# Six block slots in the last pass of a graph network, and two split-precision layers for its first five chunks

## The reference

```python
x = layernorm(x + relu((adj @ x) @ L0_kernel + L0_bias))
u = x
for _ in range(3):
    v = mlp(adj @ u, uv weights)     # three layers, leaky ReLU (0.01) after each
    u = mlp(adj @ v, vu weights)
return layernorm(x + v)
```

## Time and profile before

| | us |
|---|---|
| time, median of 3 runs | 1171.17 |
| span of the profiled execution, first to last instruction | 1169.0 |
| outside of the span (1171.17 - 1169.0) | 2.2 |
| PE busy | 1154.0 (99%) |
| DVE busy | 738.2 (63%) |
| ACT busy | 660.8 (57%) |
| last pass (tick 1392 on), start in the trace | about 1037.9 |

### The profile page before, as it was taken

How to read it: one execution, slowest core, us unless ns; L and a number is a source line. 1 busy time by engine, 2 the same in 40 slices (tenths; PEclk the granted TensorE clock), 3 DMA queues, 4 the chain that set the end, 5 groups by cost and what they waited for, 6 DMA issues and landing times.

```text
span 1169.0 us, 13697 instructions
## 1 busy us (share of the span) xinstructions
PE 1154.0 (99%) x5236; PEld 953.1 (82%) x5236; DVE 738.2 (63%) x890; ACT 660.8 (57%) x809; POOL 0.2 (0%) x4
## 2 busy tenths in 40 slices
PE   7999999999999999999999999999999999999997
PEld 6888888888888888888888888888888888887776
DVE  7997676458564555555545756554566555658886
ACT  7765554346554555555444754554566454557885
POOL 0000000000000000000000000000000000000000
PEclk9999999999999999999999999999999999999999
DMA  9988775568466646555656736655665566569891
GB/s 383 405 299 327 244 270 192 206 215 288 124 207 209 215 161 214 198 185 180 216 180 216 250 118 216 214 173 181 210 222 188 190 205 209 193 217 362 296 323 50
DMA packets 72210, 261.60 MB, mean 224 GB/s; under 512 B 8017, under 2 KB 8657, under 8 KB 71121
## 3 DMA queue, kind: packets, MB, share of 16 engines
q1 hardware_dynamic: 72000, 260.61, 64.2%
q10 hardware_dynamic: 144, 0.13, 0.0%
HBM read 258.61 MB, written 2.10 MB: 223 GB/s over the span
## 4 chain that ended last, share of the span: by engine, by line
PE 92%; DMA 3%; DVE 2%; ACT 2%; issue 1%; SPq 0%; DVEq 0%; ACTq 0%
PE agg_ps L872 28%; PE agg_ps L865 28%; PE agg_ps L858 28%; PE pre_ps L769 4%; DMA adj_raw<-in_adj 3%; PE hid_ps L730 1%; PE hid_ps L732 1%; PE hid_ps L731 1%; DVE adj_lo L722 1%; ACT adj_hi L593 1%; PE hid_ps L791 1%; PE hid_ps L805 0%; DVE stats L606 0%; ACT hid L487 0%; ACT resid L508 0%
## 5 line engine op out<-in xcount | busy, mean ns | idle before, releaser
L722 DVE TENSOR_TENSOR adj_lo<-adj_raw,adj_hi 128x1024 fp32r<-128x1024 f32 x488 | 576.7, 1220 | 230.2 <-ACT adj_hi L593 224.0
L858 PE MATMUL agg_ps<-adj_hi,feat_hi 128*128 128x512 f32 x1532 | 607.7, 397 | 7.4 <-ACT adj_hi L593 7.4
L865 PE MATMUL agg_ps<-adj_hi,feat_lo 128*128 128x512 f32 x1532 | 598.0, 390 | 0.0
L593 ACT ACTIVATE adj_hi<-adj_raw 128x1024 fp32r<-128x1024 f32 x488 | 492.8, 1052 | 94.8 <-PE agg_ps L872 80.3
L872 PE MATMUL agg_ps<-adj_lo,feat_hi 128*128 128x512 f32 x1532 | 473.8, 390 | 0.2 <-DVE adj_lo L722 0.2
L858 PEld LDWEIGHTS agg_ps<-adj_hi,feat_hi 128*128 128x128 f32 x1532 | 288.5, 188 | 68.8 <-issue 10.2
L865 PEld LDWEIGHTS agg_ps<-adj_hi,feat_lo 128*128 128x128 f32 x1532 | 288.5, 188 | 62.2 <-issue 3.4
L872 PEld LDWEIGHTS agg_ps<-adj_lo,feat_hi 128*128 128x128 f32 x1532 | 287.8, 188 | 61.9 <-DVE adj_lo L722 1.5
L487 ACT ACTIVATE hid<-hid_ps,params 128x512 f32<-128x512 f32 (+1 forms) x80 | 54.5, 681 | 59.1 <-PE hid_ps L732 50.6
L558 ACT ACTIVATE in_hi<-part 128x512 fp32r<-128x512 f32 x24 | 15.2, 634 | 110.3 <-DVE part L711 110.3
L487 ACT ACTIVATE post<-pre 128x512 f32<-128x512 f32 x39 | 24.6, 630 | 79.8 <-DVE pre L689 79.8
(11 more groups left out here) (70 smaller groups left out, 262.2 us busy)
## 6 DMA issues: line engine op xcount, KB each, us to landing
adj_raw<-in_adj SPq DMA_DIRECT2D x472, 512.0 KB, 5.7
adj_raw<-in_adj SPq DMA_DIRECT2D x8, 1024.0 KB, 8.1
resid<-in_x SPq DMA_DIRECT2D x8, 256.0 KB, 8.0
out<-resid SPq DMA_DIRECT2D x7, 256.0 KB, 6.8
params<-in_weights SPq DMA_DIRECT2D x1, 386.0 KB, 4.7
b_row<-in_bias_rows SPq DMA_DIRECT2D x1, 128.0 KB, 5.5
out<-resid ACTq DMA_DIRECT2D x1, 128.0 KB, 2.1
out<-resid SPq DMA_DIRECT2D x1, 128.0 KB, 2.2
```

Source lines behind the costliest of these rows:

```text
L593: act.activation(adj_hi[:, plan.slot[b], i * CHUNK:(i + pieces) * CHUNK], adj_raw[:, h % RAW, 0:pieces * CHUNK], ACT.Copy).then_inc(adj_hi ...
L722: dve.tensor_tensor(adj_lo[:, plan.slot[b], slot], adj_raw[:, h % RAW, 0:pieces * CHUNK], adj_hi[:, plan.slot[b], slot].bitcast(F32), ALU. ...
L858: pe.matmul(group_bank(g), feat_hi[feats][:, tile(src, i)], adj_hi[:, plan.slot[b], piece(i)], start=start, stop=False)
L865: pe.matmul(group_bank(g), feat_lo[feats][:, tile(src, i)], adj_hi[:, plan.slot[b], piece(i)], start=False, stop=False)
```

## The change

The change has two parts. First, in the last pass two more slots hold converted blocks: the features that pass 4 has read are not needed any more, so halves of `feat_hi[0]` and `feat_lo[0]` (4 chunks each, as large as a block) become slots 4 and 5. Slot 4 is free after product 340 and slot 5 after product 346, of 384. A block of the last pass may take any of the six, and its conversion stands 20 ticks ahead of its first use instead of 12 (`LAST_LEAD`). Second, the last pass's first five chunks (40 to 44) use the new steps `LAST_PARTS`: layers one and two in parts. The three or four later chunks stay as they were. The order of the 384 products on PE is unchanged.

```diff
+SPARE = 2
-LEAD, FIRST_LEAD, FIRST_ROWS = 12, 4, 3
+LEAD, FIRST_LEAD, LAST_LEAD, FIRST_ROWS = 12, 4, 20, 3
+LAST_IN_PARTS = 5
     LAST: dict(dve_sum=0, act_in=0, pe_hid1=4, act_hid1=7, pe_hid2=7, act_hid2=9, pe_out=9, dve_pre=12,
                act_post=15, dve_stats=15, act_std=20, dve_shift=20, act_norm=24),
+    LAST_PARTS: dict(dve_sum=0, act_in=1, dve_in=2, pe_hid1=5, act_hid1=7, dve_hid=9, pe_hid2=11, act_hid2=13,
+                     pe_out=15, dve_pre=17, act_post=18, dve_stats=19, act_std=22, dve_shift=23, act_norm=25),
...
-        self.slot, self.before, holder = [], [], [None] * RING
-        for b in range(len(self.blocks)):
-            k = min(range(RING), key=lambda k: -1 if holder[k] is None else self.ends[holder[k]])
+        spare = [max(n for n, (s, part, r, c) in enumerate(self.order)
+                     if s == PASSES - 2 and part == FINISH and self.node(s, c) // TILES == k) for k in range(SPARE)]
+        self.slot, self.before, freed = [], [], [None] * RING + spare
+        for b, (s, r, c) in enumerate(blocks):
+            slots = range(RING + SPARE if s == PASSES - 1 else RING)
+            k = min(slots, key=lambda k: -1 if freed[k] is None else freed[k])
             self.slot.append(k)
-            self.before.append(holder[k])
-            holder[k] = b
+            self.before.append(freed[k])
+            freed[k] = self.ends[b]
...
-            lead = FIRST_LEAD if first < FIRST_ROWS * rows else LEAD
+            lead = FIRST_LEAD if first < FIRST_ROWS * rows else LAST_LEAD if self.order[first][0] == PASSES - 1 else LEAD
...
+        def split_block(adj, feat, b):
+            k = plan.slot[b]
+            return adj[:, k, :] if k < RING else feat[PASSES % 2][:, (k - RING) * BLOCK:(k - RING + 1) * BLOCK]
...
-                u = at(t, "dve_hid", HIDDEN)
+                u = at(t, "dve_hid", DEEP)
...
-                u = at(t, "dve_in", HIDDEN)
+                u = at(t, "dve_in", DEEP)
...
-                    dve.tensor_tensor(adj_lo[:, plan.slot[b], slot], adj_raw[:, h % RAW, 0:pieces * CHUNK],
-                                      adj_hi[:, plan.slot[b], slot].bitcast(F32), ALU.subtract).then_inc(adj_lo_ready, 1)
+                    dve.tensor_tensor(split_lo(b)[:, slot], adj_raw[:, h % RAW, 0:pieces * CHUNK],
+                                      split_hi(b)[:, slot].bitcast(F32), ALU.subtract).then_inc(adj_lo_ready, 1)
```

More of the change, by code:

```diff
@@ L39 @@
 HOLD = 3
-LEAD, FIRST_LEAD, FIRST_ROWS = 12, 4, 3
+LEAD, FIRST_LEAD, LAST_LEAD, FIRST_ROWS = 12, 4, 20, 3
 LOAD_GCN, LOAD_PARAMS = 24, 90
 W_SPLIT = 320
-IN_PARTS, TURN, LATE2, LATE, END, END2 = "in_parts", "turn", "late2", "late", "end", "end2"
+IN_PARTS, TURN, LAST_PARTS, LATE2, LATE, END, END2 = "in_parts", "turn", "last_parts", "late2", "late", "end", "end2"
+LAST_IN_PARTS = 5
 STEPS = {
@@ L196, in __init__ @@
             first = self.first_use(b)
-            free = 0 if self.before[b] is None else self.ends[self.before[b]] * TILES + i + pieces
-            lead = FIRST_LEAD if first < FIRST_ROWS * rows else LEAD
+            free = 0 if self.before[b] is None else self.before[b] * TILES + self.pieces_before(b, i + pieces)
+            lead = FIRST_LEAD if first < FIRST_ROWS * rows else LAST_LEAD if self.order[first][0] == PASSES - 1 else LEAD
             due = max(free, first * TILES + i - lead)
@@ L206, in node, with pieces_before @@
         return r if s % 2 == 0 else self.rows - 1 - r
+    def pieces_before(self, b, pieces):
+        return TILES if b in self.first_spare else pieces
     def first_use(self, b):
@@ L235, in steps_of @@
             after = len(self.units) - len(END_UNITS) - u
-            return END2 if after < 0 else END if after == 0 else LATE if after == 1 else LATE2 if after == 2 else LAST
+            return END2 if after < 0 else END if after == 0 else LATE if after == 1 else LATE2 if after == 2 \
+                else LAST_PARTS if u < self.rows * (PASSES - 1) + LAST_IN_PARTS else LAST
         return TURN if r in (0, self.rows - 1) else IN_PARTS
@@ L444, in post_of, with split_hi, split_lo @@
             return post
+        def split_block(adj, feat, b):
+            k = plan.slot[b]
+            return adj[:, k, :] if k < RING else feat[PASSES % 2][:, (k - RING) * BLOCK:(k - RING + 1) * BLOCK]
+        def split_hi(b):
+            return split_block(adj_hi, feat_hi, b)
+        def split_lo(b):
+            return split_block(adj_lo, feat_lo, b)
         def at(t, step, kinds):
@@ L591, in _ @@
                     if plan.before[b] is not None:
-                        act.wait_ge(half_used, 2 * plan.ends[plan.before[b]] + (i + pieces + 1) // 2)
-                    act.activation(adj_hi[:, plan.slot[b], i * CHUNK:(i + pieces) * CHUNK],
+                        act.wait_ge(half_used, 2 * plan.before[b] + (plan.pieces_before(b, i + pieces) + 1) // 2)
+                    act.activation(split_hi(b)[:, i * CHUNK:(i + pieces) * CHUNK],
                                    adj_raw[:, h % RAW, 0:pieces * CHUNK], ACT.Copy).then_inc(adj_hi_ready, 1)
@@ L844, in _ @@
                     for k in (k, k + 1):
-                        part_hi = adj_hi[:, plan.slot[b], k * CHUNK + cut.start:k * CHUNK + cut.stop]
+                        part_hi = split_hi(b)[:, k * CHUNK + cut.start:k * CHUNK + cut.stop]
                         pe.matmul(to, feat_hi[feats][:, tile(src, k)], part_hi, start=i % 2 == 0 and k == 0, stop=False)
@@ L872, in _ @@
                         last = pe.matmul(group_bank(g), feat_hi[feats][:, tile(src, k)],
-                                         adj_lo[:, plan.slot[b], piece(k)], start=False, stop=stop and k == i)
+                                         split_lo(b)[:, piece(k)], start=False, stop=stop and k == i)
                     last.then_inc(half_used, 1)
```

9 lines of the change are left out of this document (5 added, 4 removed).

## The result

The changed kernel takes 1187.03 us (median of 4 runs, 1186.49 to 1188.43) against 1171.16 for the kernel before. The ratio is 1.0137, 95% interval 1.0125 to 1.0150: 16 us slower. The forecast was 1185.5, between 1175 and 1193.

What follows compares the result with a forecast made beforehand. PE, busy 99% of the span, was taken to bound the kernel. Pauses of 17.7 us less 3.3 saved add 14.4 to the 1169.0 span, 1183.4; with 2.2 outside it, say 1185.5 us, likely 1175 to 1193.

Steps and rivals of the forecast that it cites:

- the slots bring nothing by themselves: Last pass: PE never waits for a converted block, so six slots pay only by making room for the parts.
- a layer in parts saves PE 0.2 us: PE, chunks 40 to 44: ten layers at 0.20 us less each, say 1.9 us in all.
- hidden operations end up on the path: Last pass: DVE gains 6.0 us of work, ACT 4.4; PE then waits for `in_lo` and `hid_lo`; chance 0.74.
- 16.0 us of work against 15.9: Chunk 43, 20 ticks: DVE needs 16.0 us, PE 15.9, so DVE has nothing to spare.
- `pre` to the conversion behind post, walked at 1.7: DVE behind `pre`: waits about 1.7 us, five times, for ACT's conversion, which stands behind `post`.
- the eight pauses: PE waits at second layers of chunks 40 to 44 except full-precision ones and first layers of 42 to 44: 17.7 us.
- the walk: Last pass: DVE's and ACT's lists followed with start-to-start times, each pause from the PE start before it; sum 17.7 us.
- chunk 42's second layer, was walked at 2.3 us: PE ahead of chunk 42's second layer: a pause of 2.3 us, with ACT late by conversions and norm.
- a rival with 0.07: PE's clock falls in the pauses: three falls at the longest add 7 us (1193), eight add 19 (1205); chance 0.07.
- 14.4 was forecast: Whole span: 17.7 us of walked pauses less 3.3 taken off PE, 14.4 us more than 1169.0.
- no pause here is walked at over 3.4 us: Last pass on PE: longest walked pause 3.4 us, used as evidence against the clock rival of chance 0.07.

Runs made afterwards that it cites:

- e1: Changed kernel with the six slots and 20-tick lead alone, all last-pass chunks in full precision: 1170.66 us, ratio 0.9997.
- c1: Changed kernel with six slots, no chunk in parts, and last-pass full-precision layers one to three one tick later on PE: 1169.07 us, ratio 0.9982.
- c2: Changed kernel with full-precision layers one tick later, only chunk 40 in parts, `hid_lo` moved earlier and post behind the conversion: 1170.91 us, ratio 0.9999.
- e4: Changed kernel with ACT's post one tick later, behind that tick's conversion: 1184.41 us, ratio 1.0117.
- e6: Changed kernel with both orders mended: `hid_lo` ahead of its tick's conversion and of statistics, post behind the conversion: 1176.57 us, ratio 1.0048.
- e8: Changed kernel with both orders mended, and layers one to three of the five chunks at 8, 13, 16 ticks instead of 5, 11, 15: 1174.83 us.
- e7: Changed kernel with 12 and 14 unread matmuls filling PE's pauses at chunk 41's second and chunk 42's first layer: 1187.88 us, ratio 1.0142.
- c3: Changed kernel with full-precision layers one tick later, chunks 40 and 41 in parts, `hid_lo` moved earlier and post behind the conversion: 1173.89 us, ratio 1.0019.
- e3: Changed kernel with `hid_lo` moved ahead of total and statistics in the same tick: 1187.79 us, ratio 1.0144.
- e5: Changed kernel with `hid_lo` one tick earlier in DVE's list, ahead of the conversion of tick 8: 1182.90 us, ratio 1.0104.
- e2: Changed kernel with the five chunks in parts alone, four slots and a lead of 12 ticks: 1190.58 us, ratio 1.0166.

## Why the prediction was right

**That PE sets the end, and the slots bring nothing by themselves:** shown. What PE loses ahead of tick 1516, 17.5 us in the trace, is what the span grows by. e1 has the slots alone, with a ratio of 0.9997.

**That a layer in parts saves PE 0.2 us:** as read. Chunk 42's second layer, without a pause and at the high clock, takes 0.68 us from 1107.09 to the next product. The layers' gain is 1.9 us against 16 of pauses. The reading of the earlier trace rows was one short: there is a fourth pause in the last pass of the kernel before, 0.4 us, for chunk 39's `hid_lo`, and it goes with the slots.

**That hidden operations end up on the path:** shown. With none, one, two and five chunks in parts, the times are 1169.1 (c1), 1170.9, 1173.9 (1172.4 where the clock stayed up) and 1176.6 us, the last three with both orders mended and with 0.5 us from the moved lines. That the reason is that DVE has nothing to spare was argued from 16.0 us of work against 15.9, and is not shown: c2 pays for one chunk alone.

**Where DVE waits for ACT:** `pre` to the conversion behind post, walked at 1.7, was 1.84 for chunk 40 and 1.65 for chunks 41 to 43. It came four times and not five: behind chunk 44's `pre` DVE has no conversion and waits 0.70 us for post. e4 takes 4.6 of these 6.8 us away by moving post. e6 shows that the order of the lists is 10.5 of the 16 us, and e8's later layers are 1.7 more. How much of the rest is the added work, and how much an order that no run tried, stays open. I had put DVE's work against PE's as the ground of it all; it is the smaller share of the loss.

**The sum.** Seven of the eight pauses were within 0.4 us of the walk. The eighth, chunk 42's second layer, was walked at 2.3 us and was 0. In the trace 4.3 us at PE's low clock came in its place and beyond, the mechanism that I had as a rival with 0.07, at two pauses. Two misses, one of each sign, and they hang together: while PE was slow, DVE caught up. 14.4 was forecast; the median grew by 15.9, and the span of the traced execution by 17.5, as it is the longest of the four. That the sum came so near is not the luck of two errors that cancel, as far as e7's executions can tell, since the low clock is worth 1 us or less. The step that was wrong is "no pause here is walked at over 3.4 us", taken as a sign that the clock holds. A pause of 2.7 us was enough, and in c3 one of 2.3. The Trainium skill, page "TensorE: Matmul & The Clock Gate", section "HAM oscillation", had said that waits between groups of matmuls can lower the clock each time. The trace agrees for two pauses of seven and not for the others (3.0 and 3.3 us at the full clock behind them); what tells them apart stays open.

**What was not foreseen:** the pauses are not eight separate ones. The walk gave each from the PE start before it, which is right for adding them up, but taken by itself each looks as if it could be removed. At chunks 41 and 42, whose layers stand closest behind one another, it can't: in e3 1.9 us taken at chunk 41 returned at chunk 42 but for 0.5, and in e5 two thirds of 3.0. At chunks 43 and 44 it can: e5's 3.2 us stayed away. PE has a part in the chain too. ACT's conversions wait for slots that PE frees, 1.05 us at 1085.28 and 1.01 at 1105.34 in the changed kernel; e2, with four slots, has the same pauses, but no run has more than six.

## What to carry to other kernels

When work moves from a full engine to "idle" ones, look at their share in that stage, then walk both lists through one unit of work with start-to-start times. Look for places where engine A's next item waits for an item of B that itself waits for A: each such turn was a wait of 1.65 to 1.84 us here, and with four slots the pauses were the same as with six. A pause at the full engine is a symptom; ask whether the lagging engine would be any earlier at its next item, and try the turns together as well as one by one. The cheap gain was elsewhere: the waits of 0.2 to 0.35 us on the full engine, which one tick more of distance took away, 1.7 to 1.9 us in all.

## What the runs showed of the hardware

- PE's low clock (granted 0.50, matmuls of 512 columns 0.43 us apart instead of 0.23) came in or behind pauses of 2.1 to 4.9 us. Neither the length nor the place decides it in these runs. Chunk 41's second layer waits 2.7 us in the changed kernel and in e2: the clock fell in the first and not in the second. Chunk 43's first layer waits 3.0 us: it stayed up in the changed kernel, e2 and e3 and fell in e5. Chunk 44's second layer waits 3.3 us: it stayed up in the changed kernel and fell in e2, e3 and e4. In e6 it stayed up behind 3.2 us. Even for one kernel it differs from execution to execution: by their times and mean clocks, c3's fell in six of eleven.
- What a fall costs depends on what PE wants next. In c3, with no pause behind it, it cost 1.6 us; where PE waits for DVE at the next layer anyway, the pause there was shorter by about as much (e7: 1.7 us instead of 3.3).
- Matmuls with a result that nobody reads filled two pauses of about 3 us, and PE's mean granted clock was higher in three of four executions (0.998 to 0.999, against 0.993 to 0.995). The time hardly changed, as PE was not what the next layer waited for.
